# A fused two-layer decoder: the context attention's weight sum and row splits at other places in their queues

## The reference

```
# layer 0, context attention: keys and values are the context rows and the sequence's own
k = concatenate([ctx, x @ wk.T]); v = concatenate([ctx, x @ wv.T])
out = softmax(q @ k.T / 16) @ v @ wo.T
# layer 1, linear context attention: its key side depends on ctx alone
k, v = split(ctx @ Wkv.T);  k = where(k > 0, k + 1, exp(k))
kv_summary = einsum('bhsd,bhse->bhde', k, v);  k_sum = k.sum(-2)
# layer 0, feed forward: weights quantised to -1, 0, 1
scale = mean(abs(w)) + 1e-5;  wq = clip(round(w / scale), -1, 1) * scale
```

## Time and profile before

| | us |
|---|---|
| median of 3 runs | 735.99 (735.14 to 736.39) |
| the profiled execution, its own time | 735.17 |
| its span, first to last instruction | 733.3 |
| TensorE busy, of the span | 650.4 (89%) |
| TensorE weight loads busy | 534.9 (73%) |
| VectorE busy | 486.5 (66%) |
| ScalarE busy | 435.2 (59%) |

### The profile page before, as it was taken

One profiled execution on the slowest core, in us unless ns is written; L12 is line 12 of the kernel. 1 busy time (PEld: TensorE's weight loads), 2 busy tenths in 40 slices (PEclk: granted clock), 3 DMA queues, 4 the chain that ended last, 5 costly groups with the idle time before them and its releaser, 6 DMA issues.

```text
span 733.3 us, 13912 instructions
## 1 busy us (share of the span) xinstructions
PE 650.4 (89%) x4832; PEld 534.9 (73%) x4833; DVE 486.5 (66%) x1091; ACT 435.2 (59%) x1124; POOL 201.6 (27%) x354
## 2 busy tenths in 40 slices
PE   7798787998998999978989999999978799999950
PEld 5566677998998899864567788888865388787840
DVE  2577777469478478448877857666556577777725
ACT  4998856358357368356878747465342356566612
POOL 2455520032000000001233444344127222222315
PEclk9999899999999999998999999999999999999985
DMA  8997000220230232410020000000195201111114
GB/s 298 383 321 219 1 1 1 90 91 1 91 91 0 91 103 103 136 37 1 1 87 1 2 1 2 1 1 1 43 427 213 65 30 51 50 50 50 49 58 138
DMA packets 32226, 62.03 MB, mean 85 GB/s; under 512 B 2500, under 2 KB 26824, under 8 KB 29928
## 3 DMA queue, kind: packets, MB, share of 16 engines
q1 hardware_dynamic: 30152, 56.04, 22.6%
q0 software_dynamic: 2016, 5.22, 2.0%
HBM read 45.80 MB, written 15.55 MB: 84 GB/s over the span
## 4 chain that ended last, share of the span: by engine, by line
PE 68%; DVE 12%; ACT 12%; issue 3%; POOL 2%; DMA 2%; SPq 0%; POOLq 0%; ACTq 0%; DVEq 0%
PE banks L1783 45%; PE bank L1783 23%; ACT arena L777 4%; DVE U_split L1253 3%; ACT U_split L796 2%; DVE mx L1207 1%; DVE wabs L1386 1%; DMA ys<-arena 1%; POOL rstd L574 1%; ACT xT L731 1%; ACT arena L842 1%; DMA w_qkv<-in_w_qkv 1%; DVE fh L1436 1%; ACT arena L950 1%; ACT arena L997 0%
## 5 line engine op out<-in xcount | busy, mean ns | idle before, releaser
L1783 PE MATMUL banks<-U_split 128*128 128x512 f32 (+1 forms) x616 | 146.7, 350 | 5.9 <-DVE U_split L1253 3.9
L1783 PE MATMUL bank<-U_split 128*128 128x256 f32 (+1 forms) x864 | 113.1, 287 | 12.4 <-DVE U_split L1253 11.7
L1783 PEld LDWEIGHTS bank<-U_split 128*128 128x128 f32 x864 | 106.7, 191 | 15.7 <-issue 7.5
L1783 PEld LDWEIGHTS banks<-U_split 128*128 128x128 f32 x616 | 96.5, 190 | 23.6 <-issue 7.9
L796 ACT ACTIVATE U_split<-arena 128x1024 fp32r (+6 forms) x122 | 97.1, 822 | 22.0 <-DVE arena L1344 11.1
L1783 PE MATMUL banks<-cst,arena 128*128 128x128 f32 (+1 forms) x594 | 90.6, 280 | 6.1 <-DVE arena L1215 3.1
L1783 PE MATMUL banks<-arena 128*128 (+4 forms) x632 | 85.3, 386 | 4.8 <-DVE arena L1201 3.9
L571 POOL TENSOR_SCALAR rstd<-mv 128x1 f32<-128x1 f32 x38 | 10.8, 285 | 263.2 <-DVE mv L1185 239.8
L1783 PEld LDWEIGHTS banks<-cst,arena 128*128 128x128 f32 (+1 forms) x594 | 69.7, 143 | 18.5 <-POOL arena L602 3.7
L1783 PEld LDWEIGHTS banks<-arena 64*128 64x128 f32 (+3 forms) x632 | 61.5, 178 | 22.5 <-issue 7.6
L1043 ACT ACTIVATE arena<-banks,dmx 128x128 f32<-128x128 f32 (+1 forms) x128 | 52.8, 423 | 38.6 <-DVE dmx L1540 38.6
(11 more groups left out here) (239 smaller groups left out, 1187.5 us busy)
## 6 DMA issues: line engine op xcount, KB each, us to landing
arena<-in_w_exp SPq DMA_DIRECT2D x8, 1536.0 KB, 14.1
xs<-arena SPq DMA_DIRECT2D x8, 1032.0 KB, 14.0
arena<-in_ctxT SPq DMA_DIRECT2D x4, 1601.0 KB, 6.8
arena<-in_ctx SPq DMA_DIRECT2D x4, 1536.0 KB
arena<-in_w_f SPq DMA_DIRECT2D x3, 1024.0 KB, 11.6
arena<-xs SPq DMA_DIRECT2D x23, 129.0 KB, 2.0
w_x<-in_w_x SPq DMA_DIRECT2D x9, 256.0 KB, 7.1
arena<-in_w_oh SPq DMA_DIRECT2D x1, 2048.0 KB, 8.6
```

The costliest lines, as they stand in the source:

```text
L1783: return nc.tensor.matmul(o, w, x, start=start, stop=stop, **k)
```

## The change

Three edits, of which none adds or removes an instruction. The row sum `wabs` of batch b is taken at the head of batch b + 1 and no longer after step 4's `x_low` (the code's `c == 5`). ScalarE splits part 1 of the context rows right behind part 0, ahead of `b_exp`, and no longer in step 1. Both engines split part 2 one step earlier: ScalarE in step 2, VectorE behind `x_low` of step 2 and no longer of step 3. VectorE's place for part 1 stays.

```
-RSTEPS = (0, 1, 3)
+RSTEPS = (0, 1, 2)
 # ScalarE
                 c_split_rows(0)
+                c_split_rows(1)
                 b_exp(2 * b)
...
-                    if c in RSTEPS:
-                        c_split_rows(RSTEPS.index(c))
+                    if c == RSTEPS[2]:
+                        c_split_rows(2)
 # VectorE
             for b in range(B):
+                if b > 0:
+
+                    v.tensor_reduce(wabs[:, b - 1:b], w_f32[:, b - 1, :], AX, ALU.add,
+                                    apply_absolute_value=True).then_inc(G["w_abs"], 1)
                 b_max(2 * b, features=0 if b else 3)
...
-                    if c == 5 and b < 3:
-                        v.tensor_reduce(wabs[:, b:b + 1], w_f32[:, b, :], AX, ALU.add,
-                                        apply_absolute_value=True).then_inc(G["w_abs"], 1)
```

## The result

The changed kernel takes 731.85 us (median of 5 runs, 731.01 to 733.66), the kernel before 735.81 in the same comparison: a ratio of 0.9954 (95% interval 0.9935 to 0.9973). That is 4.0 us less, between 2.0 and 4.8. The profiled execution of the changed kernel took 733.66, with a span of 731.8.

What follows compares the result with a forecast made beforehand. TensorE was taken to wait for VectorE's low parts ahead of steps 4 and 5 in the batch loop. Batches 0 to 3 at -1.48, -1.72, +0.10 and +1.32 summed to -1.78 us: 734.2, range 732.6 to 736.0.

Steps and rivals of the forecast that it cites:

- The tail: Start of step 4's product to end of products: without the row sum -1.38 us in batch 0, -1.22 in 1 and 2.
- rival 4: The gaps ahead of steps 4 and 5 belong to the low parts' three buffers and stay: +2.0 us, 738.0; 4%.
- the rule on consistent bubbles: Trainium skill: repeating gaps on the engine to saturate can mean too little SBUF or PSUM; by it 738.0 us.
- The run: VectorE, step 2's `x_features` to step 4's `x_low`: 10.07 to 9.57 us; batch 1's step 4 product 0.50 earlier.
- The head: Row sum at batch start: free in batch 1; in 2 and 3 exponents 1.81 us late, step 4's product +1.32.
- Rival 1: Heads of batches 2 and 3 delay step 4's product by the full 1.81 us: sum -0.8, 735.2; 20%.
- rival 3: The head's lateness in batches 2 and 3 is absorbed: sum -5.4 us, 730.6; 8%.
- Step 3: Batch 1's step 3 product starts 0.58 us later, hidden by the 1.48 us TensorE stood behind it anyway.
- rival 2: Step 3's product, not step 4's, decides each batch's end: sum +1.4 us, 737.4; 9%.

Runs made afterwards that it cites:

- experiment 5: The changed kernel with 17 extra matmuls ahead of batch 1's first key projection; 736.82 us, ratio 1.0012 to the kernel before.
- experiment 6: The kernel before with 12 extra matmuls ahead of batch 1's first key projection; 736.30 us, ratio 1.0001 to the kernel before.
- experiment 8: The kernel before with the row sum behind the second maximum of the same batch, row splits as before; 731.85 us, ratio 0.9950.

## Why the prediction was wrong

The verdict faster was right, and each step in the loop held.

- **The tail.** Forecast 4.45 in batches 1 and 2 and near 4.1 in batch 0; measured 4.45, 4.46 and 3.97. The row sum did stand between `x_low` and TensorE, and the bubble did not belong to the three buffers: with the buffers as they were, 1.55 us went to 0.26. That ends rival 4 and the time that followed from the rule on consistent bubbles. A small gap stays ahead of step 5 (0.26, forecast as within 0.3).
- **The run.** The product of step 4 was to come 0.50 earlier in batch 1. The row splits alone gave 0.52 there, and 0.53 and 0.52 in batches 2 and 3.
- **The head.** Batch 1's cost nothing, as said. In batches 2 and 3 the bottom line was +0.04 and +1.27 against +0.10 and +1.32. The last maximum of batch 2 came 1.75 us later behind batch 1's products (220.34 - 183.71 against 220.52 - 185.64), forecast 1.78. The new gap on TensorE is 1.05 us, not 1.3. Rival 1 (paid in full, batches 2 and 3 at +0.6 and +1.8) and rival 3 (absorbed, -1.7 and -0.5) both fall.
- **Step 3.** Its product started with a new gap of 0.39 in batch 1 and 0.85 and 0.88 in batches 2 and 3; I had 0.6 and 1.1. It does not decide: from it to the end took 181.20 + 2.51 - 177.27 = 6.44 in batch 1, not rival 2's 7.52.
- **What failed** is one sentence of the reckoning and what stood on it: "the stages behind the loop start when it ends, so the sum should pass to the end whole", with "no term below comes from the clock". I had looked at the granted clock inside the loop, where it is whole, and not where the loop's end moves to. Behind the loop it falls to its lower level in both traces of the kernel before and costs 7.00 - 5.60 = 1.4 us at the value products. The change does not touch them, but it brings them 2 us nearer to the loop's start, and there the clock stays whole. Experiments 5 and 6 show this: put the loop's old length back, and the low clock and the old time are back; make the kernel before 1.4 us longer, and the value products get the whole clock and the time stays.

Over all executions the changed kernel's mean is 4.0 us under the kernel before's (732.2 against 736.2): 2.0 from the loop, 1.4 from the value products behind it as both pairs of traces have them, and a rest of about 0.6. Part of the rest has a place in one trace: at the second place behind the loop the changed kernel's second trace is 66.41 - 65.64 = 0.77 us shorter than its first. How often that is so is not shown. A straight line through all executions, time against mean clock with one constant for each kernel, gives 2.7 us (standard error 0.3) to the changed kernel at equal mean clock and the remainder to the clock, so part of the rest may be the chance of which executions had which clock. That stays open, as does why the clock falls at the value products for some lengths of the loop (183.15 and 179.13) and not for others (177.59, 181.15 to 182.12, and 184.53).

The rows of the trace that should have warned me were there: from 312 to 318 us the clock is 0.72, 16 us behind the last product that I reckoned, and from 328 to 342 it is 0.76. The range was too narrow by these items. With 1.4 us for one of the two places it would have held the result; with both the honest width is 2.8 us.

## What to carry to other kernels

Before a sum is passed on to the end of the kernel, look at the granted clock of the stages behind it: a stretch of low clock next to short gaps is a term of either sign for any edit that changes when that stage begins, and here it was 1.4 us at each of two places against an edit of 2.0. When variants are timed, compare their stretches in the trace beside the totals. The mean clock of each execution helps, but it does not tell the place: the changed kernel's first trace has 0.968 with the value products at the whole clock, and experiment 8's has 0.971 with them at the low one. Two parts whose totals don't add up are a sign of such a term, and padding with harmless matmuls back to the old length tests it. And before an instruction is moved off a busy place, list the waits of its engine in the whole period: the 3.7 us hole behind the second maximum was in the same timeline, and the row sum placed there is worth 3.6 us of loop more than at the head of the next batch.

## What the runs showed of the hardware

The same gap of 1.18 us stands ahead of the same 45 matmuls in all ten traces. They took 7.00 to 7.15 us in four and 5.60 or 5.61 in six. The changed kernel with and without the 17 extra matmuls of experiment 5, some 160 us ahead of them, took 7.00 and 5.60. The clock's fall is thus not a property of the gap alone. Nor does their place in the span decide: they started at 312.24, 314.74, 315.26 and 316.69 us with the low clock, and at 312.11, 314.36 and 319.08, among others, without it. The Trainium skill ("TensorE: Matmul & The Clock Gate", section "What's actually happening") says that a monitor sets the gate by how busy TensorE has been recently, and that throttled is the default which activity lifts. These traces agree in so far as the falls come where TensorE has gaps: 0.98 and 1.18 us ahead of the value products, 1.51 and 1.67 us around the second place. But two gaps of 1.5 us in 5 us within the loop never brought one; the clock is whole from 97 to 296 us in every trace.

2 us of extra matmul work cost 4.6 us in experiment 5, and 1.4 us of it cost nothing that the times show in experiment 6. VectorE's 128x2048 row sum takes 2.27 or 2.28 us at all three places where it was put.
